# A one-core decoder layer: the output product moved ahead of u's turn, projections issued a slot earlier, x and the cross queries sent sooner

## The reference

```
x = layernorm(x + attn(x; wq, wk, wv, wo, biases))        # softmax over 128 keys, 16 heads
x = layernorm(x + xattn(ctx, x, ctx; Wk, Wq, Wv, Wo))     # queries from x, keys and values from ctx
x = layernorm(x + ffn(x))                                 # int8-like: scales from min and max of ALL of x, then of all of gelu(h)
```

## Time and profile before

| | |
|---|---|
| median of 3 runs | 350.71 us (348.93 to 351.52) |
| the profiled execution's own time | 353.96 us |
| its span, first to last instruction | 352.2 us |
| DVE, PE, ACT, POOL busy, share of the span | 89%, 76%, 72%, 53% |
| attention, slots -5 to 67 | up to about 274 us |
| feed-forward | 275 to 352 us |

### The profile page before, as it was taken

How to read it: one execution, slowest core, us unless ns; L and a number is a source line. 1 busy time by engine, 2 the same in 40 slices (tenths; PEclk the granted TensorE clock), 3 DMA queues, 4 the chain that set the end, 5 groups by cost and what they waited for, 6 DMA issues and landing times.

```text
span 352.2 us, 12362 instructions
## 1 busy us (share of the span) xinstructions
PE 268.1 (76%) x4897; PEld 171.5 (49%) x4899; DVE 314.9 (89%) x720; ACT 252.9 (72%) x502; POOL 187.7 (53%) x382
## 2 busy tenths in 40 slices
PE   3679887999999999999979998888884366101980
PEld 2446654666666666666656655555552122001560
DVE  5756889899999999999979999999988599998994
ACT  2134886789889888888878888888752499604865
POOL 6233878666766666667665667766222005500285
PEclk9999999999999999999999999999985586855796
DMA  1352323132333333333323233332000000000034
GB/s 52 88 156 74 93 81 86 56 112 80 104 110 86 102 93 97 106 86 103 108 80 98 79 105 104 99 88 80 4 2 1 2 0 0 0 0 0 2 90 149
DMA packets 48992, 25.13 MB, mean 71 GB/s; under 512 B 6440, under 2 KB 48808, under 8 KB 48936
## 3 DMA queue, kind: packets, MB, share of 16 engines
q1 hardware_dynamic: 46936, 23.76, 23.4%
q10 hardware_dynamic: 2000, 0.59, 0.7%
HBM read 9.39 MB, written 2.10 MB: 33 GB/s over the span
## 4 chain that ended last, share of the span: by engine, by line
DVE 33%; PE 28%; issue 13%; POOL 12%; ACT 5%; DMA 4%; SPq 3%; ACTq 0%; POOLq 0%; DVEq 0%; another core or an unknown queue 0%
DVE neg_max L858 15%; PE ps L1091 8%; PE ps L1119 6%; DVE h_ext L966 5%; DVE h_ext L967 4%; DMA arena_h<-parts_sk 3%; SPq L409 3%; POOL rstd L541 2%; PE ps L1194 2%; PE ps L1182 2%; PE ps L1137 2%; DVE arena_q L850 2%; PE ps L1144 2%; PE ps L1159 1%; POOL o_root L608 1%
## 5 line engine op out<-in xcount | busy, mean ns | idle before, releaser
L858 DVE TENSOR_REDUCE neg_max<-ps 128x8 f32<-128x1024 f32 x128 | 157.1, 1228 | 16.4 <-PE ps L1091 13.8
L662 ACT ACTIVATE probs<-ps 128x1024 f32<-128x1024 f32 x64 | 65.6, 1025 | 17.5 <-PE ps L1098 14.9
L671 ACT ACTIVATE probs<-ps 128x1024 f32<-128x1024 f32 x64 | 65.5, 1024 | 8.8 <-PE ps L1098 8.7
L1091 PE MATMUL ps<-arena_h 31*128 31x128 f16 x1024 | 53.0, 222 | 24.5 <-DVE neg_max L858 14.4
L1091 PEld LDWEIGHTS ps<-arena_h 31*128 31x128 f16 x1024 | 31.0, 95 | 57.7 <-DVE neg_max L858 34.7
L1098 PE MATMUL ps<-arena_h 32*128 32x128 f16 x1024 | 52.1, 220 | 0.5 <-ACT probs L662 0.5
L538 POOL TENSOR_TENSOR var_eps<-mean_var,eps_col 128x1 f32<-128x1 f32 x64 | 12.2, 191 | 73.0 <-DVE mean_var L842 73.0
L1119 PE MATMUL ps<-probs,arena_q 128*32 128x128 f32 x1024 | 42.5, 285 | 0.9 <-ACT u_sb L681 0.9
L1119 PE MATMUL ps<-probs,arena_h 128*32 128x128 f32 x1024 | 42.1, 283 | 0.0
L541 POOL TENSOR_TENSOR rstd<-var_eps,minus_half 128x1 f32<-128x1 f32 x64 | 35.2, 550 | 5.0
L1098 PEld LDWEIGHTS ps<-arena_h 32*128 32x128 f16 x1024 | 29.8, 94 | 1.5 <-issue 0.9
(11 more groups left out here) (155 smaller groups left out, 641.1 us busy)
## 6 DMA issues: line engine op xcount, KB each, us to landing
arena_h<-parts_sq SPq DMA_DIRECT2D x48, 64.0 KB, 2.3
arena_h<-parts_ck SPq DMA_DIRECT2D x48, 64.0 KB, 2.2
arena_h<-parts_cq SPq DMA_DIRECT2D x48, 64.0 KB, 2.0
arena_h<-parts_sk SPq DMA_DIRECT2D x45, 64.0 KB, 2.0
xT_in<-in_xT_dram SPq DMA_DIRECT2D x16, 128.0 KB, 2.5
xN_in<-in_xN_dram SPq DMA_DIRECT2D x16, 128.0 KB, 2.5
cT_in<-in_cT_dram SPq DMA_DIRECT2D x16, 128.0 KB, 2.4
cN_in<-in_cN_dram SPq DMA_DIRECT2D x16, 128.0 KB, 2.2
```

What stands on the lines that cost most here:

```text
L662: act.activation(probs[1][:, :], ps_s2, ACT.Exp, scale=SCALE).then_inc(ex, 1)
L671: act.activation(probs[0][:, :], ps_s2, ACT.Exp, scale=SCALE).then_inc(ex, 1)
L858: dve.tensor_reduce(neg_max[b.par][:, HH * half:HH * half + HH], ps_s1.rearrange("p (h k) -> p h k", h=HH), AXX, ALU.max, negate=True).the ...
L1091: ins = pe.matmul(ps_s1[:, at:at + S], q[r:r + MAX_AT, j, :], kk[r:r + MAX_AT, j, :], start=True, stop=True, skip_group_check=True)
```

## The change

On TensorE the output product of x moves from behind `product(1)` to ahead of the turns of u, and writes the third quarter of bank 5 instead of bank 7; bank 7 (`ps_p`) is left to the projections. DVE no longer waits for the output product by itself; its wait for u's turn covers it. From slot 2 on the projections of slot k+1 are issued at the end of slot k, where those of slot k stood ahead of `scores(1)`; they wait for the evacuation of the projections of slot k. In slot 2 the old place is used as well. `xT` of pairs 6 and later is loaded 11 slots ahead instead of 8. The cross queries are split and filled in the slot max(C - 8, S + 8) instead of C - 4 (C, S: the first positions of the pair): that is 4 slots sooner for pairs 2 to 13, 2 slots for pairs 1 and 14, none for 0 and 15. The keys ck stay at C - 4.

```
+XT_LATER_AT, CQ_AT, X1_TURNED = 11, 8, 8
...
+def xT_pairs(k):
+    ahead = [(i, XT_AT if i < LEAD_PAIRS else XT_LATER_AT) for i in range(LOADS, PAIRS)]
+    return [i for i, at in ahead if S_POS[2 * i] - at == k]
+def cq_pairs(k):
+    return [i for i in range(PAIRS) if max(C_POS[2 * i] - CQ_AT, S_POS[2 * i] + X1_TURNED) == k]
...
-        ps_o = bank(7)
+        ps_o = ps_t[:, 2 * S:3 * S]
+        ps_p = bank(7)
...
# SyncE, slot(k), behind the fills of sq, ck and sk
-                if cross_fill is not None:
-                    fill("cq", Q_PARTS, cross_fill)
+                for i in cq_pairs(k):
+                    ring_free(C_POS, i)
+                    fill("cq", Q_PARTS, i)
+                for i in xT_pairs(k):
+                    load_xT(i)
...
# GpSimd, slot(k), behind the split of sk
-                i = C_FIRST.get(k + FILL_AT)
-                if i is not None:
+                for i in cq_pairs(k):
                     pool.wait_ge(txe, 2 * i + 2)
                     split(pool, "cq", cq_full[i % RING][:, :], i)
...
# VectorE, slot(k)
                 if x is not None:
-                    dve.wait_ge(oo, x.pos + 1)
+                    if w is None:
+                        dve.wait_ge(oo, x.pos + 1)
...
# TensorE
-                def projections():
+                def projections(k):
                     q, kk, vv, ck = q_pair(k), k_pair(k), S_FIRST.get(k + V_AT), C_FIRST.get(k + CK_AT)
                     if projections_at(k) is not None:
-                        need(pe, yy, tasks_to(k - 4))
-                    waited = task(k - 4) is not None
+                        past_q, past_k = q_pair(k - 1), k_pair(k - 1)
+                        if past_k is not None:
+                            pe.wait_ge(eqk, 2 * past_k + 2)
+                        elif past_q is not None:
+                            pe.wait_ge(eqk, 2 * past_q + 1)
+                        for first, at, n in ((S_FIRST, V_AT, evv), (C_FIRST, CK_AT, eck)):
+                            i = first.get(k - 1 + at)
+                            if i is not None:
+                                pe.wait_ge(n, i + 1)
...
                     pe.transpose(ps_x[0:H, S:2 * S], neg_max[nxt.par][:, :], ident[:, :]).then_inc(mt, 1)
+                if w is not None and w.pos == 1:
+                    pe.wait_ge(w_step, 2)
+                if x is not None:
+                    if nxt is None:
+                        pe.wait_ge(tae, x.pos + 1)
+                    need(pe, yy, x.pos)
+                    pe.matmul(ps_o, attT[:, :], (wo_self if x.kind == "S" else wo_cross)[:, :],
+                              start=True, stop=True, skip_group_check=True).then_inc(oo, 1)
                 if w is not None:
...
                     last.then_inc(tu, 1)
-                if k >= LEAD_SLOTS:
-                    projections()
+                if k == LEAD_SLOTS:
+                    projections(k)
                 scores(1)
                 product(1)
...
-                if x is not None:
...
-                    pe.matmul(ps_o[:, 0:D], attT[:, :], (wo_self if x.kind == "S" else wo_cross)[:, :],
-                              start=True, stop=True, skip_group_check=True).then_inc(oo, 1)
...
                     pe.transpose(ps_x[:, 2 * S:3 * S], x1_all[:, v.m, :], ident[:, :]).then_inc(tx, 1)
+                if k >= LEAD_SLOTS:
+                    projections(k + 1)
```

More of the change, by code:

```diff
@@ L454, in slot @@
                     fill("sk", K_PARTS, self_fill)
-                if cross_fill is not None:
-                    fill("cq", Q_PARTS, cross_fill)
-                for at, first, load in ((XT_AT, S_FIRST, load_xT), (XN_AT, S_FIRST, load_xN),
-                                        (CT_AT, C_FIRST, load_cT), (CN_AT, C_FIRST, load_cN)):
+                for i in cq_pairs(k):
[3 more added lines that the diff above has]
+                    load_xT(i)
+                for at, first, load in ((XN_AT, S_FIRST, load_xN), (CT_AT, C_FIRST, load_cT), (CN_AT, C_FIRST, load_cN)):
                     i = first.get(k + at)
-                    if i is not None and not (load is load_xT and i < LOADS) and not (load is load_xN and i == 0):
+                    if i is not None and not (load is load_xN and i == 0):
                         load(i)
@@ L893, in slot @@
                             dve.wait_ge(xb, x.pair + 1)
-                        dst, own, residual = y_sb[x.place][:, :], ps_o[:, 0:D], x_bias[x.ring][:, x.half, :]
+                        dst, own, residual = y_sb[x.place][:, :], ps_o, x_bias[x.ring][:, x.half, :]
                     else:
-                        dst, own, residual = (by_group(y_sb[x.place][:, :]), by_group(ps_o[:, 0:D]),
+                        dst, own, residual = (by_group(y_sb[x.place][:, :]), by_group(ps_o),
                                               in_groups(x1_all[:, x.m, :]))
@@ L1134, in projections @@
                         pe.wait_ge(s_xT[q % LOADS], landed(q, LOADS))
-                        if not waited:
-                            need(pe, evv, q)
-                        last = pe.matmul(ps_o[:, 0:PAIR], wq_g[:, :], xT_in[q % LOADS][:, :], start=True, stop=True,
+                        last = pe.matmul(ps_p[:, 0:PAIR], wq_g[:, :], xT_in[q % LOADS][:, :], start=True, stop=True,
                                          skip_group_check=True)
@@ L1141, in projections @@
                     if kk is not None:
-                        if q != kk and not waited:
-                            pe.wait_ge(eqk, 2 * kk + 1)
-                        pe.matmul(ps_o[:, PAIR:2 * PAIR], wk_g[:, :], xT_in[kk % LOADS][:, :], start=True, stop=True,
+                        pe.matmul(ps_p[:, PAIR:2 * PAIR], wk_g[:, :], xT_in[kk % LOADS][:, :], start=True, stop=True,
                                   skip_group_check=True).then_inc(pqk, 2 if q == kk else 1)
@@ L1148, in projections @@
                             pe.wait_ge(w_v, 16)
-                        if not waited:
-                            pe.wait_ge(eqk, 2 * vv + 2)
                         for half in range(2):
-                            last = pe.matmul(ps_o[:, half * D:(half + 1) * D], xT_in[vv % LOADS][:, half * S:(half + 1) * S],
+                            last = pe.matmul(ps_p[:, half * D:(half + 1) * D], xT_in[vv % LOADS][:, half * S:(half + 1) * S],
                                              wv_sb[:, :], start=True, stop=True, skip_group_check=True)
```

24 lines of the change are left out of this document (5 added, 19 removed).

## The result

The changed kernel takes 353.02 us (median of 15 runs, 351.45 to 354.35), the kernel before 350.51 on the same chips (15 runs, 348.81 to 352.57): ratio 1.0064, interval 1.0043 to 1.0085. It is 2.5 us slower. The forecast was 348.8 with a range to 351.6, so it missed in direction and by 4.2 us.

What follows compares the result with a forecast made beforehand. DVE was taken to bound attention. Terms +1.2 - 1.8 - 1.5 - 0.7 made -2.8 against the profiled 353.96; with half of B, -1.9 against the median 350.71: 348.8, own range 347.4 to 350.3, with rivals 345.8 to 351.6.

Steps and rivals of the forecast that it cites:

- POOL's new wait: Slots 48 and 50: split of cq waits for ck of an earlier pair; covered by 1.3 us, at most 1.5 us lost.
- rival 4: POOL's wait in slots 48 and 50 reaches DVE, +1.5 us, giving 350.3; chance 0.07.
- Term A: Regular slots 12 to 61: product ahead of u's turns makes the reciprocal late, first half 1.79 us; +1.2 us in all.
- rival 1: Regular slots: the reciprocal isn't late, first half falls to 1.73, A is -1.6 instead of +1.2, giving 346.0; chance 0.18.
- Term B: Cross queries filled sooner in slots 12 to 47 remove PE's 1.9 us wait: -1.8 in this execution, -0.9 on the median.
- rival 3: Projection at a slot's end makes scores(0) late by 0.08 us in 41 slots, +3.3, giving 352.1; chance 0.08.
- Term C: Last slots: DVE's waits for the output product in slots 62 and 64 go, the reciprocal comes 0.21 later; -1.5 us.
- Term D: First slots: earlier projections release DVE from POOL's clearing memsets sooner; -0.7 us, bounds +0.4 and -1.4.
- Rival 5: First slots: the shared-port lock is given up between memsets, D at -1.2, giving 348.3; chance 0.03.
- x sooner: SP's earlier loads of xT, needed by the earlier projections: about 1 us later in slot 3, costing nothing.

Runs made afterwards that it cites:

- a_cq12late: The changed kernel with splits and fills of cq of pairs 12 and later back at four slots ahead of use: 347.12 us, ratio 0.9884 to before.
- b_cq: The kernel before with only the splits and fills of cq up to four slots sooner, old TensorE order and loads of x: 356.73 us, ratio 1.0145.
- a_cqlast: The changed kernel with SyncE's fills of cq behind the loads of xT, xN, cT and cN in each slot: 349.90 us, ratio 0.9985 to before.
- j_projections: From a_cqlate, projections stay at the slot's end, output product back behind product(1), where it also waits for att: 359.90 us, ratio 1.0242 to before.
- d_sq: From c_clear, SP sends the fills of sq five slots ahead, sk stays at four: 346.89 us, ratio 0.9876 to before.
- c_clear: From a_cq12late, GpSimd's clearing of cross rings 0 to 2 moved to slot -2, ring 3 to slot 1: 344.85 us, ratio 0.9835 to before.
- p_product: From a_cqlate, output product stays ahead of u's turn, projections back ahead of scores(1) of their own slot: 359.55 us, ratio 1.0246 to before.
- b_clear: The kernel before with only the clearings moved, cross rings 0 to 2 to slot -2, ring 3 to slot 1: 348.77 us, ratio 0.9944.
- a_cqlate: The changed kernel with splits and fills of cq of every pair back at four slots ahead: 347.60 us, ratio 0.9895 to before.
- a_sems: The changed kernel with separate semaphores for the stacks of ck and cq: 349.14 us, ratio 0.9943 to before.
- a_sems_early: As a_sems, but PE's wait for ck's stack a slot earlier, ahead of product(1) of the slot before: 347.96 us, ratio 0.9929 to before.

## Why the prediction was wrong

**The step that failed is "POOL's new wait".** It names the right place and mechanism (rival 4), has the root of slot 49 one microsecond into the slot, finds it covered by 1.3 us, and allows 1.5 at most. Measured: 5.4 us in the stretch, and 1.8% between the ratios of the changed kernel and a_cq12late (6.3 us). Added to the forecast change of -1.9, the 5.4 alone make a loss of 3.5; the chance given to rival 4 was 0.07, and its price 1.5. Three things in its sizing were wrong:

- SP's time for ck 10 was read from before (issues from 205.06, 0.3 us ahead of slot 48) and kept. But "in slots 12 to 47 each slot keeps the same number of splits and fills" is false for slot 46, where the fills of cq 11 are one stack more (in a_cq12late, which keeps them, SP starts ck 10 1.5 us into the slot). After, SP starts ck 10 2.0 us into the slot and its last issue is 4.3 into it. The landing comes 6.4 us into the slot (GpSimd starts at 207.65), and the root of slot 49 is begun 3.9 us after the start of slot 49, where I had 1.0. Cover 1.3, need 2.9.
- It asked what is queued behind the split on POOL, but not on SP, where the fills of cq wait for that split and cT stands behind them. TensorE waits 2.0 us for cT.
- The change itself moves the projection of ck, which needs cT, from the middle of its slot to the end of the one before, ahead of `scores(0)`. Under the old order (b_cq) there is no wait for cT, and the stretch loses 3.85 instead of 5.44; a_cqlast puts 0.9 of that difference on cT. I judged the parts one by one, and these two add up.

**Term A** (forecast +1.2): the mechanism was right to two hundredths (turn at 0.80, reciprocal at 1.22) and the last addend wrong. The 0.59 from reciprocal to reduction in slot 59 is not what DVE needs. It ends on PE's scores, which begin 1.27 us after the reduction before and let DVE start 0.46 later, 1.73, in slot 59 as in after; statistics and att fit into 0.51. So the first half fell to 1.73, the price of rival 1 without its condition, since the reciprocal is late. It shows in slots 12 to 46: the 34 first halves take 1.1 us less together (1.3 without slot 43, which is long by 0.2), and the second halves 1.2: the landing of term B gives 1.75, and landings of sk in slots 35 and 39 take 0.6 back. The read of y ends 0.88 us ahead of the next product, not 0.67, which changes nothing. The second half stays at 1.73 to 1.77 as forecast, and rival 3 is out. j_projections shows how near it was: 0.2 us of work more in that half and it is 1.98.

**Term B** (forecast -0.9 on the median): there is indeed no wait for cross queries from 76 to 250 us. But a wait of the same size stands in slot 9, for pair 0, so the net between the two traces is nothing. That one isn't made by the change: b_cq, with the old order, has it at 1.9 us. Of the nine traces with the clearings in their place eight have it, at 1.2 to 1.9 us, and of the four with the clearings moved only d_sq. GpSimd's split of that cq begins 2.4 us into slot 8 in after, behind the memsets, and 0.9 us in c_clear. The two traces without it, before and p_product, have TensorE wait 2.0 and 1.6 us for sk in slot 7 instead; GpSimd goes on meanwhile, and its split begins 0.7 and 1.6 us into slot 8. I had not asked what is late next once a late landing stays away. The wait at 180 us, on which B rested, came back in no trace at that place; the others have one of 0.2 to 1.7 us elsewhere or none, so it was the chance of one execution.

**Term C** (forecast -1.5): -1.68. Right, with its cause: the two waits are gone and the one for u's turn grew from 0.78 to 1.01. The old order itself varies here: b_cq takes 23.24 us from slot 61 on, b_clear, with one of the two waits, 22.29.

**Term D** (forecast -0.7, bounds to -1.4): -1.90, and -2.7 in a_cqlate, outside the bounds. But these are differences from a trace with 2.0 us of a late landing in slot 7. Against b_cq, the same program as before up to there, the new order with the clearings in place is 0.1 to 0.6 us shorter from slot 2 to slot 9 in after and the five kernels made from it that keep its order of TensorE, inside the bounds. Whether the old place of the projections makes such a landing likelier is open: of the three traces with it and the clearings in place, before and p_product wait 1.6 us or more in slot 7 and b_cq 0.3; those with the new place wait under 0.5. That the memsets hold DVE is shown by c_clear and b_clear. What a release by half a microsecond is worth was not tried by itself. Rival 5 is answered by the same rows. In after both chains begin ahead of L865 (49.04 and 49.19; 56.58 and 56.69), and L865 is held for 2.10 and 1.39 us, to the end of the chain or of its second memset, never only for the one that was running (0.95). The Trainium skill, "SBUF — State Buffer", section "SBUF: two separate sides", has the lock held for one instruction; by that L865 would have started at 49.99 and ended 1.0 us sooner than it did in slot 5. The measurement differs, and it decides. The row with 2.42 us in the prediction is a case of the same kind: ahead of the first memset (50.54) GpSimd was at the split, in before:

```profile
49.93 0.67 POOL L376 TENSOR_TENSOR parts_sq<-q_full,parts_sq 128x256 f16<-128x256 f32 x1
```

so L850, begun at 50.37, also began behind a running instruction of GpSimd, and was held over the whole chain, of five memsets and not four.

**x sooner** cost nothing that shows: TensorE has no wait for xT in slots 12 to 61.

The sum with what was measured in the traces is -1.9 - 2.3 + 5.4 - 0.1 - 1.7 = -0.6 up to the extremes, where the forecast for the profiled execution was -2.8. It doesn't meet the +2.5 between the medians, because before's execution was 3.45 above its median, with at least two late landings of 2 us in it. The ratios do meet: the new order without sooner cq is worth -1.05% (a_cqlate), 3.7 us, the stretch takes 5.4 back, and +1.7 stands against the measured +0.64%, 2.2 us. Reading gains off an execution that is a per cent above its median overstates them; I halved B for it, but took the rest in full.

## What to carry to other kernels

When a step is moved to an earlier place, write down for its first and last instances, where the schedule leaves its rhythm, what it waits for and when that is issued. A semaphore shared by two streams makes the moved one wait for the other. And follow each wait over every queue that it blocks, SP's too, down to what another part of the same change has made urgent. Before a gap of one trace is priced, look for it in a second trace of the same program: of the two largest landings of before, the one at 180 us is in no other trace here and the one in slot 7 in one of thirteen.

A gap at the end of a chain shows what that chain's consumer needs only if the consumer was not waiting for another engine. And where an exchange of two pieces of work is proposed, each half-loop's budget on each engine has to be written out: here one of two pieces fits, and both together cost some 0.25 us a slot.

## What the runs showed of the hardware

A fourth semaphore that an instruction of TensorE waits for put its start off by 0.16 us though it had been reached long before (1.45 against 1.29 us after the reduction, in some 15 places); with three it started at 1.29. The Trainium skill, "Perfetto Trace Analysis", section "Identifying Dependency Chains", says that instructions which wait on several engines may get extra semaphore instructions ahead of them. The trace agrees: a_sems has 12371 instructions, a_sems_early and a_cq12late 12355, and the 16 more are semaphore instructions of TensorE, one for each cross pair. In the half shown above two of them stand ahead of L1113 in a_sems, where a_cq12late has one.

DVE's tensor_scalar from SBUF to SBUF stands through whole chains of GpSimd memsets (2.42 and 2.32 us before, 2.10 and 2.15 elsewhere, against 0.34 alone), but ended 1.39 us (after) and 1.33 us (a_cq12late) after its start, behind the second memset, in some cases. What decides between the two was not tried.

Three fills of 64 KB, issued at the same point of the same program, were usable 5.0 us after their first issue in one execution (before) and 3.2 in another (b_cq).
